# Forget attention's set-up moved to the end of the first experts stage, its value ring cleared by place, its first eight x groups turned into another bank

## The reference, cut to what matters

```
x = x + attention_a(layernorm(x))      # 16 heads of 16, rotary, softmax
x = x + experts(layernorm(x))          # top 8 of 64 experts, a shared expert
x = x + forget_attention(layernorm(x)) # below
x = x + experts(layernorm(x))          # the same weights again

# forget_attention, per head, over the 16 steps of the sequence:
q, k, v = h @ Wq.T + bq, h @ Wk.T + bk, h @ Wv.T + bv
phi_q, phi_k = elu(q) + 1, elu(k) + 1
f = sigmoid(h @ Wf.T + bf)
S = f * S + outer(phi_k, v);  z = f * z + phi_k
out = (phi_q @ S) / (phi_q @ z + 1e-6)
return out @ Wo.T + bo
```

## Time and profile before

| | us |
|---|---|
| median of 3 runs | 2708.31 (2702.72 to 2710.55) |
| the profiled execution | 2699.52 |
| its span, first to last instruction | 2697.9 |
| TensorE busy / VectorE / ScalarE / GpSimd | 2424.7 / 1739.1 / 1266.7 / 1128.3 |
| first instructions of forget attention | 1656.87 |
| its first result added (L1653) | 1730.9 |
| its last | 2175.0 |

### The profile page before, as it was taken

One profiled execution on the slowest core, in us unless ns is written; L12 is line 12 of the kernel. 1 busy time (PEld: TensorE's weight loads), 2 busy tenths in 40 slices (PEclk: granted clock), 3 DMA queues, 4 the chain that ended last, 5 costly groups with the idle time before them and its releaser, 6 DMA issues. The chain is left out here.

```text
span 2697.9 us, 47073 instructions
## 1 busy us (share of the span) xinstructions
PE 2424.7 (90%) x14506; PEld 1332.6 (49%) x14506; DVE 1739.1 (64%) x3661; ACT 1266.7 (47%) x2564; POOL 1128.3 (42%) x1350
## 2 busy tenths in 40 slices
PE   8996899999999999799889993899999979898885
PEld 5653133333333333266557662566666556556663
DVE  7996888888888888188422222688888759632221
ACT  3553477666767767444223230555555424322221
POOL 6888100000010000133236663677777713226765
PEclk9998799999999999899989995999999989998998
DMA  5555332333323331155848862011111036766883
GB/s 167 187 180 172 107 95 87 91 94 91 98 83 94 91 89 56 50 176 184 256 137 227 204 148 55 13 39 38 37 37 33 21 116 203 234 190 185 202 203 53
DMA packets 289375, 325.31 MB, mean 121 GB/s; under 512 B 28945, under 2 KB 270753, under 8 KB 289185
## 3 DMA queue, kind: packets, MB, share of 16 engines
q1 hardware_dynamic: 257536, 274.49, 33.6%
q0 software_dynamic: 27136, 46.16, 8.5%
q10 hardware_dynamic: 4512, 2.40, 0.4%
HBM read 217.23 MB, written 105.19 MB: 120 GB/s over the span
## 5 line engine op out<-in xcount | busy, mean ns | idle before, releaser
L720 ACT ACTIVATE a_probs<-a_ps_s 128x512 f32<-128x512 f32 x1024 | 537.0, 602 | 284.7 <-PE a_ps_s L597 272.4
L672 DVE TENSOR_REDUCE a_row_max<-a_ps_m 128x2 f32<-128x1024 f32 x512 | 607.6, 1219 | 89.6 <-PE a_ps_m L571 85.4
L597 PE MATMUL a_ps_s<-a_qs,a_ks 98*128 98x512 bf16 (+1 forms) x1024 | 319.5, 391 | 8.6 <-ACT a_probs L720 7.3
L612 PE MATMUL a_ps_o<-a_probs,a_va 128*32 128x512 f32 x2048 | 273.2, 606 | 0.8 <-ACT a_o_sb L729 0.8
L1538 POOL TENSOR_TENSOR b_spread<-b_decay,held_own_sb 128x512 f32<-128x512 f32 x256 | 269.3, 1086 | 8.2 <-DVE b_weight L1636 8.2
L571 PE MATMUL a_ps_m<-a_ks,a_qs 48*128 48x512 bf16 x1024 | 207.2, 402 | 17.2 <-DVE a_row_max L672 11.5
L546 POOL DMA_DIRECT2D x<-a_xo x32 | 23.5, 734 | 437.3 <-DVE a_xo L705 437.3
L571 PEld LDWEIGHTS a_ps_m<-a_ks,a_qs 48*128 48x128 bf16 x1024 | 49.3, 93 | 311.2 <-issue 191.0
L1636 DVE TENSOR_TENSOR b_weight<-b_ps_s,b_spread 128x512 f32<-128x512 f32 x256 | 163.8, 682 | 17.6 <-PE b_ps_s L1773 17.6
L597 PEld LDWEIGHTS a_ps_s<-a_qs,a_ks 98*128 98x128 bf16 (+1 forms) x1024 | 76.2, 97 | 166.9 <-ACT a_probs L720 75.5
L517 POOL CAST a_high<-a_row_max 128x32 bf16<-128x32 f32 x32 | 6.7, 209 | 320.2 <-DVE a_row_max L672 320.2
(11 more groups left out here) (350 smaller groups left out, 5273.7 us busy)
## 6 DMA issues: line engine op xcount, KB each, us to landing
parts<-a_parts SPq DMA_DIRECT2D x16, 1536.0 KB, 6.2
a_qs<-parts SPq DMA_DIRECT2D x384, 64.0 KB, 2.2
a_ks<-parts SPq DMA_DIRECT2D x384, 64.0 KB, 2.2
rows<-m_early SPq DMA_DIRECT2D x32, 640.0 KB, 3.2
m_early<-x SPq DMA_DIRECT2D x32, 512.0 KB, 4.0
m_own<-in_L_ffn_w_gate_dram SPq DMA_DIRECT2D x24, 384.0 KB, 4.3
m_own<-in_L_ffn_w_up_dram SPq DMA_DIRECT2D x24, 384.0 KB, 5.7
m_own<-in_L_ffn_w_down_dram SPq DMA_DIRECT2D x24, 384.0 KB, 6.6
```

Source lines behind the costliest of these rows:

```text
L597: nc.tensor.matmul(s_bank(name, step)[:], ks[u][0:K_ALL[e], h, t * P:(t + 1) * P], qs[u][0:K_ALL[e], h, :], start=True, stop=True).then_in ...
L612: last = nc.tensor.matmul(ps_o[VW * j:VW * (j + 1), :], va[n.u][:, t, (h0 + j) * VW:(h0 + j + 1) * VW], probs[:, group % 2, j, t, :], star ...
L672: nc.vector.tensor_reduce(row_max[:, n.k // 4 % 2, t, :, n.p % 4], m_bank(name, step)[:], AX.X, ALU.max).then_inc(m_drained, 1)
L720: nc.scalar.activation(probs[:, group % 2, j, t, :], s_bank(name, step)[:], ACT.Exp, scale=DK ** -0.5).then_inc(s_drained, 1)
```

## The change

Three edits.

1. The masks, the bias terms and the turned weights are made by the first experts stage (tag m1), behind all of that stage's other work on TensorE, ScalarE and VectorE. They go to held tiles; each weight is turned in its own tile, in place. ScalarE now copies the turned banks out, not VectorE. `w_qk` becomes a pair of tiles.
2. The ring `v_aug` is cleared one group at a time by `clear_values` on GpSimd at lag 1, with two memsets for each of the first 12 groups, and no longer at once.
3. The first RAMP = 8 groups are transposed by `turn_early` into `ps_w` (free until the first outputs), at lag 1, first in TensorE's step; ScalarE's `evacuate_early` copies them out. Groups from 8 on go as before. `project_values` waits for its own group and for the previous group's gates to be copied.

```
 # moe_experts, behind in_turn(...)
+            def turn_b_weights(i):                       # tensor
+                if i < 2:
+                    pe.wait_ge((xT_done, hT_done)[i], PAIRS)
+                wait(pe, w_copied, i - 1)
+                bank = (ps_x, ps_t)[i % 2]
+                for c in range(2):
+                    if i < 4:
+                        for r in range(2):
+                            last = nc.tensor.transpose(bank[:, c, r, :], b_w[i][:, r * D + c * P:r * D + (c + 1) * P], ident[:])
+                    else:
+                        last = nc.tensor.transpose(bank[:, c, 0, 0:H], f_rows[:, c * P:(c + 1) * P], ident[0:H, 0:H])
+                last.then_inc(w_turned, 1)
+            if prepares:                                 # tag == "m1"
+                for i in range(5):
+                    turn_b_weights(i)
+            def keep_b_weights(i):                       # scalar
+                act.wait_ge(w_turned, i + 1)
+                bank = (ps_x, ps_t)[i % 2]
+                if i < 3:
+                    nc.scalar.activation(b_w[i][:].rearrange("p (c a) -> p c a", c=2), bank[:].rearrange("p c r a -> p c (r a)"), ACT.Copy).then_inc(w_copied, 1)
...
+            if prepares:                                 # vector: the 19 instructions of L1549 to L1572, into held tiles
+                nc.vector.tensor_reduce(odd_even[:], head_rows[:].rearrange("p (i j) -> p j i", j=2), AX.X, ALU.add).then_inc(masks_done, 1)
...
 # forget_attention, gpsimd
-            nc.gpsimd.memset(v_aug[:], 0.0).then_inc(setup, 1)
-            pool.wait_ge(setup, 3)
-            nc.gpsimd.memset(v_aug[:, :, :, DK:DK + 1], 1.0).then_inc(setup, 1)
+            pool.wait_ge(setup, 2)
+            def clear_values(n):
+                if n < VB:
+                    nc.gpsimd.memset(v_aug[:, n, :, DK:DK + 1], 1.0).then_inc(cleared, 1)
+                    nc.gpsimd.memset(v_aug[:, n, :, DK + 1:], 0.0).then_inc(cleared, 1)
-            in_turn([(0, inverse_deviation), (L_UPTO, log_gates), ...
+            in_turn([(0, inverse_deviation), (1, clear_values), (L_UPTO, log_gates), ...
 # vector: L1549 to L1583 removed
 # scalar
-            act.wait_ge(masks_done, 13 + HALVES + 2 * (TERMS - 1))
-            act.wait_ge(setup, 4)
+            def evacuate_early(n):
+                if n < RAMP:
+                    act.wait_ge(x_turned, n + 1)
+                    nc.scalar.activation(xnT[:, n // SG % 2, :, n % SG * P:(n % SG + 1) * P], ps_w[:, 0:2, :], ACT.Copy).then_inc(xnT_done, 1)
             def evacuate_values(n):
                 act.wait_ge(vf_ready, n + 1)
+                if n < VB:
+                    act.wait_ge(cleared, 2 * (n + 1))
-            in_turn([(L_VF, evacuate_values), ...
+            in_turn([(L_TURN - 1, evacuate_early), (L_VF, evacuate_values), ...
 # tensor: L1718 to L1729 removed
             def project_values(n):
-                pe.wait_ge(xnT_done, min(n + L_VF - L_TURN, GROUPS))
+                pe.wait_ge(xnT_done, n + 1)
+                wait(pe, f_copied, n)
+            def turn_early(n):
+                if n < RAMP:
+                    pe.wait_ge(xn_done, n + 1)
+                    wait(pe, xnT_done, n)
+                    for c in range(2):
+                        last = nc.tensor.transpose(ps_w[:, c, :], xn[:, n % 4, c * P:(c + 1) * P], ident[:])
+                    last.then_inc(x_turned, 1)
             def turn_x(n):                               # and evacuate_x
+                if n >= RAMP:
                     ...
             def turn_output(n):
+                pe.wait_ge(xnT_done, RAMP)
-            in_turn([(L_VF, project_values), (L_S, scores), (L_PV, mix_values), (L_TURN, turn_x), (L_OUT, turn_output), (L_FEED, first_features), ...
+            in_turn([(L_TURN - 1, turn_early), (L_VF, project_values), (L_S, scores), (L_PV, mix_values), (L_TURN, turn_x), (L_OUT, turn_output), (L_FEED, first_features), ...
 # held_constants: tiles b_w_q, b_w_k, b_w_o, b_w_v in place of b_w_rows; tiles for the masks and terms
```

More of the change, by code:

```diff
@@ L1348, in _ @@
             in_turn([(L_DOWN, copy_second), (L_TURN, copy_x), (L_GU, silu(0)), (L_GU, silu(1)), (L_TURN_H, copy_h)])
+            def keep_b_weights(i):
[3 more added lines that the diff above has]
+                    nc.scalar.activation(b_w[i][:].rearrange("p (c a) -> p c a", c=2), bank[:].rearrange("p c r a -> p c (r a)"), ACT.Copy).then_inc(w_copied, 1)
+                elif i == 3:
+                    nc.scalar.activation(b_w[3][:].rearrange("p (c a) -> p c a", c=2)[:, :, 0:D], bank[:].rearrange("p c r a -> p c (r a)"),
+                                         ACT.Copy).then_inc(w_copied, 1)
+                else:
+                    for half in range(2):
+                        dst = b_w[3][:].rearrange("p (c a) -> p c a", c=2)[:, :, D:VF].rearrange("p c (r h j) -> p c r h j", r=4, h=2)[:, :, :, half, :]
+                        last = nc.scalar.activation(dst, bank[:, :, 0, half * 8:half * 8 + 8].rearrange("p c (r j) -> p c r j", j=2), ACT.Copy)
+                    last.then_inc(w_copied, 1)
+            if prepares:
+                for i in range(5):
+                    keep_b_weights(i)
         @block.vector
@@ L1418, in sem @@
             return nc.alloc_semaphore("b_" + name)
[L1420 to L1424, removed]
+        w_q, w_k, w_o, w_vf = (const["b_w_" + m][:].rearrange("p (c a) -> p c a", c=2) for m in "qkov")
+        w_qk = (w_q, w_k)
         ident = const["ident_sb"]
@@ L1738, in project_values @@
                 last.then_inc(vf_ready, 1)
-            def turn_x(n):
-                pe.wait_ge(xn_done, n + 1)
-                wait(pe, f_copied, n + L_TURN - L_VF + 1)
-                wait(pe, xnT_done, n)
-                wait(pe, decay_done, n + L_TURN - L_UPTO)
-                for c in range(2):
-                    last = nc.tensor.transpose(ps_a[:, c * P:(c + 1) * P], xn[:, n % 4, c * P:(c + 1) * P], ident[:])
-                last.then_inc(x_turned, 1)
+            def turn_early(n):
[5 more added lines that the diff above has]
+                    last.then_inc(x_turned, 1)
+            def turn_x(n):
+                if n >= RAMP:
+                    pe.wait_ge(xn_done, n + 1)
+                    wait(pe, f_copied, n + L_TURN - L_VF + 1)
+                    wait(pe, xnT_done, n)
+                    wait(pe, decay_done, n + L_TURN - L_UPTO)
+                    for c in range(2):
+                        last = nc.tensor.transpose(ps_a[:, c * P:(c + 1) * P], xn[:, n % 4, c * P:(c + 1) * P], ident[:])
+                    last.then_inc(x_turned, 1)
             def sum_logs(n):
@@ L1805, in project_out @@
                 last.then_inc(out_ready, 1)
-            in_turn([(L_VF, project_values), (L_S, scores), (L_PV, mix_values), (L_TURN, turn_x), (L_OUT, turn_output), (L_FEED, first_features),
+            in_turn([(L_TURN - 1, turn_early), (L_VF, project_values), (L_S, scores), (L_PV, mix_values), (L_TURN, turn_x), (L_OUT, turn_output), (L_FEED, first_features),
                      (L_UPTO, sum_logs), (L_OUT, turn_att), (L_FEED, last_features), (L_OUT, project_out)])
@@ L1837, in held_constants @@
     ahead.append((down[0:SF - P, 1, :], a["L0_ffn_ws_down"][P:SF, :]))
-    w_rows = hold("b_w_rows", [P, 8, D])
-    for i, m in enumerate("qkvo"):
-        ahead.append((w_rows[:, 2 * i:2 * i + 2, :], rows(a["L0_attn_b_W" + m])))
+    for i, m in enumerate("qkov"):
+        w = hold("b_w_" + m, [P, 2 * D if m != "v" else 2 * (D + STEPS)])
+        ahead.append((w[:, 0:2 * D].rearrange("p (c d) -> p c d", c=2), rows(a["L0_attn_b_W" + m])))
     ahead.append((hold("b_f_rows", [STEPS, D])[:], a["L0_attn_b_Wf"]))
```

123 lines of the change are left out of this document (51 added, 72 removed).

## The result

The changed kernel takes 2694.88 us in the median of 20 runs (2680.41 to 2716.13). The kernel before, run beside it, takes 2709.23 in the median of 20 (2696.07 to 2733.72). The ratio is 0.9947, with a 95% interval of 0.9925 to 0.9969, so the change is faster by about half a per cent.

The account below looks back on a forecast made before the run. Forget attention's steady part was taken as TensorE-bound at full clock, its beginning not. Terms of 9.9 + 4.8 - 3.8 - 4.2 gave 6.7 us less, 2701.6 from the median 2708.31; range 2696 to 2708.5.

Parts of the forecast that it names:

- Term 1: Start of forget attention: with the set-up and its memset gone, first statistics wait only for x; 9.9 us less.
- Term 2: First statistics to first Relu of forget attention: early transposes shorten the fill from 20.66 to 15.9 us, 4.8 less.
- Term 3: Steps 7 and 8: early transposes stand first on TensorE and wait for VectorE's normalise; 1.9 us each, 3.8 more.
- Term 4: Steps 7 and 8: TensorE's clock falls to half after pauses of 4.0 us; 2.1 us each, 4.2 more.
- A: Steps 7 and 8: the clock does not fall in the pauses; gain 10.9 us, time 2697.4; chance 20%.
- B: End of the experts stage: moved work holds up GpSimd's scatters, at most 4.0 us back, say 2704.5; chance 10%.
- C: Ramp of forget attention: the clock stays at half; slower, 2712.7 with two further feature blocks at half clock; chance 6%.
- D: Start of forget attention: the stage or its first loads wait for something unseen; no change, 2708; chance 4%.

Follow-up runs that it names:

- with the clock held: The changed kernel plus four useless TensorE products ahead of each early transpose of groups 6 and 7, order kept: median 2696.7 us, ratio 0.9959.

## Why the prediction was right or wrong

**What the change gives.** Three measurements of it gave ratios of 0.9947, 0.9989 and 0.9943. Weighted by their intervals they are 0.9958 with half an interval of 0.0015, which is 11.5 us less (give or take 4). Three traces of before and three of the change, by the length of forget attention alone: 522.2, 524.2, 525.1 against 514.1, 512.1, 514.6, means of 523.8 and 513.6, or 10.2 less. The forecast had 6.7. All of it arises ahead of the third Relu, as the forecast said. The sign of being wrong that the forecast named, a first result more than 11 or less than 2 us earlier, did not come: it was 8.2 in the profiled pair and 10.3 in the means.

**Term 1, the set-up: right, but for a small cost where the work went.** Forecast -9.9, measured 12.86 to 2.62 in the means, -10.2. The next thing late is x, as said. That the work fits behind the experts is shown too: from VectorE's last copy of a product there (1626.56) to forget attention's start (1654.99) it is 28.4 us, 25.5 and 28.5 in the other two traces of the change, where it was 28.1 (1628.82 to 1656.88), 28.3 and 26.1 in the three traces of before. The timeline of the changed kernel shows the moved work there:

```profile
1626.56 0.42 DVE L1424 COPY m1e_y<-m1e_ps_y 128x256 f32<-128x256 f32 x1 [3.86 <-PE m1e_ps_y L1328]
...
1627.10 0.16 DVE L1434 TENSOR_SCALAR held_b_minus_qk<-held_b_qk 128x4 f32<-128x4 f32 x1
...
1629.32 0.26 ACT L1387 ACTIVATE held_b_w_v<-m1e_ps_x 128x16 f32<-128x16 f32 x2
...
1630.68 1.55 POOL L1277 DMA_INDIRECT x<-m1e_y,m1e_slots  x1 [3.77 <-DMA x<-m1e_y,m_slots]
1630.83 0.42 DVE L1454 CAST held_b_terms<-m1e_b_rest 32x528 bf16<-32x528 f32 x1
```

It is done 4.7 us behind that copy (1631.25), 23.7 us ahead of the stage's end. But GpSimd's round of scatters in that place is longer than its counterpart in the kernel before:

```profile
1628.11 1.55 POOL L1268 DMA_INDIRECT x<-m1e_y,m_slots  x1 [0.30 <-issue]
1632.56 1.55 POOL L1268 DMA_INDIRECT x<-m1e_y,m1e_slots  x1 [2.90 <-DMA x<-m1e_y,m_slots]
1634.42 1.55 POOL L1268 DMA_INDIRECT x<-m1e_y,m_slots  x1 [0.30 <-issue]
```

From the first of these to the last it is 6.3 us; in the first trace of the change 7.2 (1625.35 to 1632.54), with a wait of 3.77 in place of 2.90. In the three traces of before and the one with the set-up put back this round takes 6.3 to 6.4; in the nine traces that have the moved work it takes 6.4 to 7.2, 6.7 in the mean; the rounds just ahead of it and behind it take 6.3 to 6.5 in all. As each scatter waits for the one before and what follows is as long as ever, the stage ends some 0.4 us later for it.

**Term 2, the fill: right mechanism, too small.** Forecast -4.8, from 20.66 to 15.9. In the first pair of traces it is 15.46, -5.2. The parts, forecast and measured: first values at 5.6 and 5.1; three values intervals 7.0 and 7.4; last values to the Relu 3.3 and 3.0. The memsets by place cost GpSimd 0.12 and 0.29, together inside the 0.2 to 0.6 that was bounded. But the fill of before is not always 20.7: the other two traces have 21.2 and 22.1, and those of the change have 14.6 and 14.5. The means are 21.3 and 14.9, so the term is -6.4, near the end of its bounds (-6.7).

The lengths go with the moment at which the clock rises. These are windows on its two sides in the first and in the second trace of the change (columns as above):

```profile
1655.00:1667.30 12.30, 6.24 (x18) 4.15 (x19) 6.18 (x20) 3.24 (x7) 7.20 (x28) 0.50 0.63 178
1667.40:1673.00 5.60, 4.73 (x19) 2.61 (x17) 0.94 (x4) 1.93 (x8) 0.12 (x1) 1.00 0.09 27
```

```profile
1667.90:1678.40 10.50, 4.48 (x13) 2.71 (x13) 6.17 (x20) 2.88 (x7) 6.61 (x26) 0.50 0.63 175
1678.50:1685.00 6.50, 5.60 (x23) 3.47 (x23) 0.94 (x4) 2.19 (x9) 0.51 (x3) 1.00 0.27 79
```

From the stage's start to the rise it is 12.3, 10.5 and 9.7 us in the three traces of the change, with fills of 15.5, 14.6 and 14.5; in those of before it is 31.8, 32.8 and 34.7, with fills of 20.7, 21.2 and 22.1. The working had the clock rise between the second and the third group of values. That is so in the first trace of the change; in the other two it is up when the second group starts.

**Term 3, the new order: right place, 0.4 too large each.** Forecast 1.9 for each step, and 1.7 as its lower bound; with the clock held it is 1.46 and 1.48. The chain of waits is the forecast's; its links overlap more than was added up. From the transpose to the features' products it is 1.31 with the clock held (1688.15 to 1689.46), not 0.41 + 1.20 = 1.6, and from the features' end (1676.51) to the transpose (1676.89) it is 0.38, not 0.33 + 0.15. So the lower bound of 1.7 was too high as well.

**Term 4, the clock: right.** Forecast +4.2. Both pauses came (3.91 against 4.0), and the clock fell behind both in all three traces of the change. With the order at 2.94, the half clock is 19.03 - 14.65 = 4.4 in the profiled execution, and 4.4 in the mean of three (19.1).

**Terms 3 and 4 against the kernel before: the step that failed.** Together they were +8.0, and the working set them against a kernel before in which the clock stays up through these steps ("no pause of these steps was over 1.5"). That is true of the trace that was read: intervals of 5.64 and 6.07, and +7.3 measured in that pair. In the other two traces of before the clock falls in step 8, so the mean of the two intervals together is 12.7 and not 11.7, and the difference is +6.4. The working looked at the pause of 1.50 alone; the transpose behind it is followed by another of 0.74, and behind the two of them the clock falls in three of four executions, two of before and the one without early turns. Behind the same two pauses in step 7 it stays up in all four.

**The account.** In the means the sum is -10.24 - 6.43 + 6.35 = -10.32, the first result shows -10.3 (75.7 to 65.4), and the stage's length -10.2. In the pair of profiled executions it is -10.3 - 5.2 + 7.3 = -8.2, and the first result shows -8.2. So the account is closed in both. The forecast's 6.7 was 3.6 too small. The one trace of before that was read accounts for 1.6 of that (its fill is 0.6 and its two steps are 1.0 shorter than the means), the earlier rise of the clock in the fill of the change for 1.0, the new order, sized too large, for 0.9, and the set-up for 0.3; the clock of term 4 goes 0.2 the other way.

**The range.** Taken off 2708.31, a gain of 10.3 gives 2698.0, and 2698.4 with the 0.4 at the experts' tail: inside the range. The first median lies over 3 below that, and no term holds this part; it is within the scatter of medians. The forecast's own starting point, 2708.31 of three runs, is borne out by later medians (2709.23, 2706.95, 2710.76, 2709.61). But single runs of one kernel have a standard deviation of 6 to 10 us here, and a median of 12 or 20 of them still moves by several: the same changed kernel gave 2694.88, 2705.16 and 2697.87, two of them inside the range. The working knew only that three runs of before spread over 8. Its lower end of 2696 stood 5.6 below the forecast; the best ends of the sum alone, 13.2 less or 2695.1, reach lower, and the spread of a median had to be added to that.

**The rivals.** A, that the clock does not fall in the pauses, is refuted by all three traces of the change. The measured time lies near A's 2697.4 by chance, and only the trace tells the two apart. B, that the moved work costs time at the experts' tail, is refuted in its size, up to 4.0 us: the tail is some 0.4 us longer (above). The Trainium skill's page "DMA: Bandwidth & Descriptors", section SWDGE vs HWDGE vs iDMA, gave the reason for B: VectorE in a two-port mode keeps GpSimd from writing the descriptors of its DMAs. The 0.4 us agree with a small cost of that kind, but no run here shows that this is its cause. C is refuted: the clock is at 1.00 from the third Relu on. D is refuted by the start: 2.6 in place of 12.9.

**Left open.** What makes the first experts stage 258.9 us long in one trace and 287.9 in another was not tried; it is the larger part of the scatter. Why the clock rises up to 2.6 us sooner in one execution of the change than in another is not shown.

## What to carry to other kernels

A gain in a pipeline's fill can be given back where the new order puts an instruction of TensorE behind a result that another engine makes late in the step: count the pause, and count the half clock behind it as a second price. Turning ahead only the groups whose normalise is not queued behind features (six here and not eight) kept the gain and removed the price of the order, and all but one fall of the clock. And a forecast from one execution takes over whatever state that execution happened to be in: read the same stretch in a second trace of the unchanged kernel before setting a range.

## What the runs showed of the hardware that was not expected

- The clock fell behind shorter pauses than the rows of before suggested: behind one of 2.65 us, and in two of three traces of the kernel before behind 1.50 and 0.74 us with a transpose between them, while in the third the same pauses left it up, as they did one step earlier in all three. So the same instructions of the same kernel take 1.10 us in one execution and 2.04 in another.
- Two useless products in the time when x is on its way did not bring the clock up sooner: it rose 12.0 us behind the stage's start with them, 11.8 and 10.4 in the two kernels with six early groups without them. They left the fill where it was, whereas the ones put into pauses later held it at 1.00.
- GpSimd's memset of 5.23 us held VectorE's small operation for 5.06 us, but statistics of 256 elements ran beside it in 0.43. Nothing here tells what makes the difference.
